# Three score buffers and one working bank in an attention and coupling block

## The reference

```
q, k, v, g = x @ Wq.T, x @ Wk.T, x @ Wv.T, x @ Wg.T      # 16 query heads, 4 key/value groups, head size 8
v = v * sigmoid(g);  q, k = rms_norm(q), rms_norm(k);  q, k = rotary(q), rotary(k);  q = q * q_gain
for s in (first half of the head, second half):           # head size 4 each
    a[s] = softmax(causal(q[s] @ k[s].T / 2)) @ v[s]
y = concat(a[0] - lam * a[1], a[0] + lam * a[1])
x = layernorm(x + y @ Wo.T)                               # over all 16 sequences
gf = global_net(mean of x over the tokens)                # three small dense layers
out = x
for _ in range(3):
    tf = coupling_net(out)                                # dense 128-128-64-32-1, gelu, sigmoid at the end
    out = out + (0.1 + adaptive_range * (0.7 * gf + 0.3 * tf - 0.5) * 2) * twist(out)
result = layernorm(x + out)
```

## Time and profile before

| | before |
|---|---|
| median of three runs | 305.38 us (305.05, 305.38, 306.28) |
| the profiled execution | 305.05 us |
| its span, first to last instruction | 303.2 us |
| TensorE matmuls busy | 270.1 us |
| ScalarE busy | 237.7 us |
| VectorE busy | 199.9 us |
| GpSimd busy | 82.4 us |
| mean granted TensorE clock | 0.991 |

### The profile page before, as it was taken

One profiled execution on the slowest core, in us unless ns is written; L12 is line 12 of the kernel. 1 busy time (PEld: TensorE's weight loads), 2 busy tenths in 40 slices (PEclk: granted clock), 3 DMA queues, 4 the chain that ended last, 5 costly groups with the idle time before them and its releaser, 6 DMA issues.

```text
span 303.2 us, 8211 instructions
## 1 busy us (share of the span) xinstructions
PE 270.1 (89%) x2888; PEld 119.0 (39%) x2888; DVE 199.9 (66%) x764; ACT 237.7 (78%) x337; POOL 82.4 (27%) x241
## 2 busy tenths in 40 slices
PE   4069899999999999999999999999998999998990
PEld 3042343434434344344443444434343322222890
DVE  5577467676676765767657677563244567799884
ACT  2158889898898988989889898897875777776565
POOL 6331231513315133141431414321011000042263
PEclk9999999999999999999999999999999999999996
DMA  4204235161442506426053340632200156533025
GB/s 107 64 1 91 53 67 105 41 138 27 94 97 78 104 19 136 89 49 139 17 104 82 81 98 17 121 75 53 64 0 1 45 132 138 125 85 69 27 76 177
DMA packets 56918, 23.40 MB, mean 77 GB/s; under 512 B 42656, under 2 KB 53824, under 8 KB 56896
## 3 DMA queue, kind: packets, MB, share of 16 engines
q1 hardware_dynamic: 56896, 23.12, 34.2%
HBM read 4.90 MB, written 2.10 MB: 23 GB/s over the span
## 4 chain that ended last, share of the span: by engine, by line
PE 45%; DVE 25%; ACT 13%; issue 11%; POOL 2%; DMA 1%; DVEq 0%; POOLq 0%; SPq 0%; ACTq 0%
PE S L661 6%; PE MA L373 5%; ACT probs_past L809 5%; PE O L560 5%; PE O L553 5%; PE S L448 5%; PE MA L586 3%; PE S L487 3%; DVE cY L1246 3%; DVE square L988 2%; PE S L478 2%; DVE turned L997 2%; ACT probs_late L809 2%; DVE heads L1110 2%; ACT qkvg L787 2%
## 5 line engine op out<-in xcount | busy, mean ns | idle before, releaser
L809 ACT ACTIVATE probs_late<-S 128x1024 f32<-128x1024 f32 x64 | 62.5, 1038 | 8.2 <-PE S L458 8.2
L809 ACT ACTIVATE probs_past<-S 128x1024 f32<-128x1024 f32 x64 | 62.1, 1024 | 6.4 <-PE S L448 5.2
L809 ACT ACTIVATE probs_early<-S 128x1024 f32<-128x1024 f32 x32 | 31.0, 1021 | 8.4 <-PE S L487 8.4
L547 PE MATMUL O<-probs_past,values 128*32 128x512 f32 x256 | 34.5, 611 | 0.7
L553 PE MATMUL O<-probs_late,values 128*32 128x256 f32 x512 | 34.3, 385 | 0.0
L1342 POOL TENSOR_TENSOR minus_half_sum<-sum_eps,minus_half 128x40 f32<-128x40 f32 x16 | 4.3, 268 | 104.2 <-DVE estimate L1016 104.2
L1025 DVE TENSOR_TENSOR roped<-rotated,rstd 128x128 f32<-128x128 f32 x64 | 12.2, 250 | 30.9 <-POOL rstd L1357 30.9
L1246 DVE SCALAR_TENSOR_TENSOR cY<-coup,ratio,Y 128x256 f32<-128x256 f32 x48 | 25.1, 565 | 7.9 <-ACT coup L891 7.9
L458 PE MATMUL S<-qk 32*64 32x256 bf16 x512 | 29.4, 292 | 0.9 <-ACT probs_past L809 0.4
L661 PE MATMUL S<-X,cn_w 128*128 128x512 f32 x48 | 25.3, 629 | 1.0 <-DVE X L1252 1.0
L373 PE MATMUL MA<-w_proj,xT_in 128*128 128x224 f32 x64 | 18.9, 424 | 4.5 <-DMA xT_in<-in_xT 3.9
(11 more groups left out here) (172 smaller groups left out, 544.4 us busy)
## 6 DMA issues: line engine op xcount, KB each, us to landing
Y<-X SPq DMA_DIRECT2D x48, 128.0 KB, 2.3
xT_in<-in_xT SPq DMA_DIRECT2D x16, 128.0 KB, 2.5
x_res<-in_x SPq DMA_DIRECT2D x16, 128.0 KB, 2.1
out<-result SPq DMA_DIRECT2D x8, 256.0 KB, 2.3
qk<-parts SPq DMA_TRANSPOSE x15, 4.9
future_in<-in_future SPq DMA_DIRECT2D x1, 128.0 KB, 2.1
w_o<-in_w_o SPq DMA_DIRECT2D x2, 64.0 KB, 2.0
cn_w<-in_cn_w SPq DMA_DIRECT2D x2, 64.0 KB, 2.4
```

What stands on the lines that cost most here:

```text
L547: mm = pe.matmul(O[32 * g:32 * g + 32, :], values[p][:, 0, g, s, at:at + 32], probs_past[:, s, g, :], start=m == 0, stop=False)
L809: act.activation(dst, S[n % 2][:, :, :], ACT.Exp).then_inc(exp_done[n], 1)
```

## The change

The score tiles get a third buffer of two banks, S[2]. `TILE_BUFFER` gives each of the ten tiles its buffer and `TILE_BEFORE` the tile whose exponential has to be done before the buffer is written. The banks MA, MB and MC give way: one bank M now takes, in turn, the projection of b + 2, the turned x1 of b - 2, the turned outputs, the turned heads and the output projection of b - 1. In the stages before and after the batches MB and MA are names for the two halves of S[2], and MC for M.

A late pair is written together: both far parts, both masks, both near parts (`late_pair`). On TensorE turning x1 comes behind late pair 4, turning the outputs behind late pair 6, turning the heads behind the early pair, and the output projection behind weighing 3, at the end of the batch. Turning x1 also waits for the sum of its own batch and for the copy of the projection, turning the outputs for that copy. On ScalarE the copy of the projection comes one exponential earlier, the keeping of x1 one later, the tanh one later, and the copy of the heads one later. On VectorE the heads are normalized before the values are gated. The output projection's reader, `add_residual`, and the next projection keep their places.

```
+TILE_BUFFER = (0, 1, 2, 0, 1, 2, 0, 1, 0, 2)
+TILE_BEFORE = (8, 7, 9, 0, 1, 2, 3, 4, 6, 5)
...
-        S = [ps(f"S{i}", [128, 2, R * 128]) for i in range(2)]
+        S = [ps(f"S{i}", [128, 2, R * 128]) for i in range(3)]
         O = ps("O", [128, R * 128])
-        MA = ps("MA", [128, 512])
-        MB = ps("MB", [128, 512])
-        MC = ps("MC", [128, 512])
...
+        M = ps("M", [128, 512])
+        MB, MA, MC = S[2][:, 0, :], S[2][:, 1, :], M[:, :]
...
             def bank_free(b, n):
 
-                if n >= 2:
-                    pe.wait_ge(exp_done[n - 2], b + 1)
+                before = TILE_BEFORE[n]
+                if before < n:
+                    pe.wait_ge(exp_done[before], b + 1)
                 else:
-                    reach(pe, exp_done[len(TILES) - 2 + n], b)
+                    reach(pe, exp_done[before], b)
...
+            def late_pair(b, p, n):
+
+                for m in (n, n + 1):
+                    bank_free(b, m)
+                for m in (n, n + 1):
+                    late_part(p, m, True)
+                for m in (n, n + 1):
+                    late_mask(m)
+                for m in (n, n + 1):
+                    late_part(p, m, False).then_inc(scores_done[m], 1)
...
-            def turn_outputs(b):
+            def turn_outputs(b, project_more, bank=M):
 
                 pe.wait_ge(n_["o_ready"], b + 1)
                 reach(pe, n_["X0_ready"], b if not isinstance(b, int) or b < BATCH - 1 else b - 1)
+                if project_more:
+                    pe.wait_ge(n_["qkvg_ready"], b + 4)
...
-            def turn_x1(b, bank=MB):
+            def turn_x1(b, project_more, bank=M):
 
                 pe.wait_ge(n_["x1_ready"], b + 1)
+                reach(pe, n_["summed_done"], b + 1)
+                if project_more:
+                    pe.wait_ge(n_["qkvg_ready"], b + 5)
...
                 weigh(b, p, 0)
-                late_first(b, p, 4)
+                late_pair(b, p, 4)
                 if not first and not second:
-                    turn_x1(b - 2)
-                late_rest(b, p, 4)
+                    turn_x1(b - 2, project_more)
                 weigh(b, p, 1)
+                late_pair(b, p, 6)
                 if not first:
-                    turn_outputs(b - 1)
-                late_first(b, p, 6)
-                late_rest(b, p, 6)
+                    turn_outputs(b - 1, project_more)
                 weigh(b, p, 2)
-                if not first:
-                    turn_heads(b - 1, project_more)
                 early_pair(b, p, 8)
                 if not first:
+                    turn_heads(b - 1)
+                weigh(b, p, 3)
+                if not first:
                     output_projection(b - 1)
-                weigh(b, p, 3)
...
                 exponentials(b, 2)
-                exponentials(b, 3)
                 if project_more:
                     copy_projection(b + 2, p)
+                exponentials(b, 3)
+                exponentials(b, 4)
                 if not first and not second:
                     keep_x1(b - 2)
-                exponentials(b, 4)
                 exponentials(b, 5)
+                exponentials(b, 6)
                 if project_more:
                     gate_tanh(b + 2, p)
-                exponentials(b, 6)
                 exponentials(b, 7)
+                exponentials(b, 8)
                 if not first:
                     copy_heads(b - 1)
-                exponentials(b, 8)
                 exponentials(b, 9)
...
+                if not first:
+                    normalize_heads(b - 1)
                 if not last:
                     gate_values(b + 1, 1 - p)
-                if not first:
-                    normalize_heads(b - 1)
```

More of the change, by code:

```diff
@@ L217, in block_kernel @@
         result = sb("result", [128, 4, 4, DIM])
-        S = [ps(f"S{i}", [128, 2, R * 128]) for i in range(2)]
+        S = [ps(f"S{i}", [128, 2, R * 128]) for i in range(3)]
         O = ps("O", [128, R * 128])
-        MA = ps("MA", [128, 512])
-        MB = ps("MB", [128, 512])
-        MC = ps("MC", [128, 512])
[L225 to L228, removed]
+        M = ps("M", [128, 512])
+        MB, MA, MC = S[2][:, 0, :], S[2][:, 1, :], M[:, :]
+        Z_BANKS = (MB, MA, O[:, :], MC)
+        BACK_BANKS = (S[0][:, 0, :], S[0][:, 1, :], S[1][:, 0, :], S[1][:, 1, :], MB, MA, O[:, :], MC)
+        TURN_BANKS = (S[2][:, 0, :].bitcast(BF16), S[2][:, 1, :].bitcast(BF16))
+        MAX_BANKS = (S[1][:, 0, :], S[1][:, 1, :])
+        MAX_TURN_BANKS = tuple(bank.bitcast(BF16) for bank in MAX_BANKS)
         names = ("w_proj_loaded gain_loaded trig_loaded ident_future_loaded w_out_loaded ffn_loaded tables_ready zeros_ready biases_halved "
@@ L372, in project, with turn_queries @@
                 for t in range(T):
-                    mm = pe.matmul(MA[:, t * PROJ:(t + 1) * PROJ], xT_in[p][:, t * 128:(t + 1) * 128], w_proj[:, :],
+                    mm = pe.matmul(M[:, t * PROJ:(t + 1) * PROJ], xT_in[p][:, t * 128:(t + 1) * 128], w_proj[:, :],
                                    start=True, stop=True)
                 mm.then_inc(n_["proj_done"], 1)
-            def turn_queries(b, t, parts_in="parts_ready", turned="turned"):
+            def turn_queries(b, t, parts_in="parts_ready", turned="turned", banks=TURN_BANKS):
                 pe.wait_ge(n_[parts_in], b + 1)
-                if t == 1:
-                    reach(pe, n_["heads_done"], b - 1)
-                bank = (MC16, MB16)[t]
+                bank = banks[t]
                 for n in range(R * 2):
@@ L395, in turn_keys @@
                     u = NQ + n * G
-                    mm = pe.transpose(MC16[:, n * 128:(n + 1) * 128],
+                    mm = pe.transpose(TURN_BANKS[0][:, n * 128:(n + 1) * 128],
                                       parts[:, u:u + G, :, :].rearrange("p u s d -> p (u s d)"), ident16[:, :])
@@ L420, in blocks_for_maximum @@
                         r, s = n // 2, n % 2
-                        bank = (MB, MC)[n % 2]
+                        bank = MAX_BANKS[n % 2]
                         for g in range(G):
@@ L467, in late_mask @@
                         rows = halves((j + h) % 2)
-                        pe.matmul(S[n % 2][halves(1 - t), j, t * 256:(t + 1) * 256], future16[rows, 0, rows], one_edge(rows, R),
+                        pe.matmul(S[TILE_BUFFER[n]][halves(1 - t), j, t * 256:(t + 1) * 256], future16[rows, 0, rows], one_edge(rows, R),
                                   start=False, stop=True)
@@ L477, in early_part @@
                             rows = group_rows(2 * h + j)
-                            pe.matmul(S[n % 2][halves(t), j, s * 256:(s + 1) * 256], kT[p][rows, t, s, halves(t)],
+                            pe.matmul(S[TILE_BUFFER[n]][halves(t), j, s * 256:(s + 1) * 256], kT[p][rows, t, s, halves(t)],
                                       qT[p][rows, t, :, s, halves(t)], start=s == 0, stop=False)
@@ L486, in early_mask @@
                         rows = halves((j + h) % 2)
-                        mm = pe.matmul(S[n % 2][halves(t), j, :], future16[rows, 0, rows], one_edge(rows, 2 * R),
+                        mm = pe.matmul(S[TILE_BUFFER[n]][halves(t), j, :], future16[rows, 0, rows], one_edge(rows, 2 * R),
                                        start=False, stop=True)
@@ L786, in copy_projection, with keep_x1 @@
                 reach(act, n_["values_ready"], b - 1)
-                act.activation(qkvg[p][:, :, :].rearrange("p t c -> p (t c)"), MA[:, 0:T * PROJ], ACT.Copy)\
+                act.activation(qkvg[p][:, :, :].rearrange("p t c -> p (t c)"), M[:, 0:T * PROJ], ACT.Copy)\
                    .then_inc(n_["qkvg_ready"], 1)
-            def keep_x1(b, bank=MB):
+            def keep_x1(b, bank=M):
                 at = b * SEQ
@@ L929, in _ @@
             gelu1(0, 1)
-            copy_heads(BATCH - 1)
+            copy_heads(BATCH - 1, MA)
             gelu2(0, 0)
@@ L1100, in subtract_maximum, with normalize_heads @@
                 dve.memset(parts[:, 0:NQ, 6, 0:3], 0.0)
-            def normalize_heads(b):
-                turned_o = MB[:, :].rearrange("p (n c) -> p n c", c=32)[:, :, 0:4 * OUTROW]\
+            def normalize_heads(b, bank=M):
+                turned_o = bank[:, :].rearrange("p (n c) -> p n c", c=32)[:, :, 0:4 * OUTROW]\
                     .rearrange("p n (w c) -> p n w c", c=OUTROW)
```

65 lines of the change are left out of this document (27 added, 38 removed).

## The result

| | before | after |
|---|---|---|
| median | 305.83 us (4 runs, 305.05 to 308.24) | 288.48 us (4 runs, 288.27 to 288.74) |
| ratio to before, 95% interval | | 0.940 (0.935 to 0.944) |
| span of the profiled execution | 303.2 us | 286.6 us |
| one steady batch | 12.72 us | 11.63 us |

The account below looks back on a forecast made before the run. TensorE was taken to bound each batch: 12.72 - 11.65 = 1.07, times 16 = 17.1 us, from 305.05 to 288.0; jitter made it 288.8, and 0.33 for the median 289. Range 286 to 298.

Parts of the forecast that it names:

- TensorE bounds, and work taken from it shows: Steady batch: TensorE busy 12.44 of 12.72 us, so issuing or waiting less shortens it, to 11.65.
- The late pair, 0.82: TensorE's late score tiles: three groups instead of five, 0.82 (0.72 to 0.95) against 1.18, saving 0.72 a batch.
- the early masks' 0.56: Early pair's eight masks of 512 columns: 0.56 taken as evidence that two mask groups share one drain.
- The walk through the waits: One new batch stepped through all engines with trace prices: next batch at 11.65, one wait of 0.17 staying.
- the wait that it named: TensorE before weighing 0, which needs the output bank copied by ScalarE: 0.17 a batch.
- The third buffer: Score tiles: no tile waits for the exponential that frees its buffer, though the first two margins are 0.1.
- only the waits go: Rival: no TensorE group gets cheaper, batch 12.37, 299 to 300 us; chance 0.08.
- The single bank M: Bank shared by projection, x1, outputs, heads and output projection: ScalarE's copies out of it are done before TensorE wants them.
- the slow rival: Bank M: each ScalarE copy slips behind one more exponential (0.92), batch 13.46, 317 us; chance 0.04.
- The ring of x1: Turning x1, output projection, VectorE's sum and x1: 11.47 a batch, margin 0.18; x1 late gives 293, chance 0.12.
- The ends: First and last batches: 0.9 to 1.3 gained, SyncE's transpose a batch ahead of use, front stage unchanged.
- The 0.8 added for jitter: Batches where three engines' cycles nearly tie: 0.05 a batch from the spread of exponentials, raising 288.0 to 288.8.

Follow-up runs that it names:

- the tile-by-tile kernel: Changed kernel with late pairs written one tile after the other again, three buffers, bank M and new order kept: 296.88 us, ratio 0.964.
- the fastest kernel: Changed kernel with both past pairs written earlier, the sum of x1 moved ahead of the split and x1 normalized inside the split: 283.52 us, ratio 0.923.
- The table of the kernels: Batch times: three buffers, merged late pairs 11.63, unmerged 12.19; two buffers, merged 14.79, unmerged 13.45; kernel before 12.72 us.
- past pair early: Changed kernel with the next batch's first past pair written ahead of the output projection: 289.68 us, ratio 0.946.
- the kernel with the second past pair first: Changed kernel with first past pair ahead of output projection, sum of x1 moved, second past pair ahead of the projection: 286.82 us, ratio 0.933.

## Why the prediction was right

**TensorE bounds, and work taken from it shows.** Right. The steady batch was forecast at 11.65 and is 11.63. Of the 1.07 to be gained the forecast had 0.72 as work and 0.35 as waits; of the 1.09 gained 0.68 was work and 0.41 waits.

**The late pair, 0.82.** Right, 0.84, and the mask group is the 0.34 that was interpolated, not the 0.24 or 0.47 of its bounds. That it shows in the batch is what the tile-by-tile kernel confirms, less the 0.12 that its longer pair hides. The prediction took the early masks' 0.56 as siding with one fixed cost for both tiles' masks. That row alone did not tell the rules apart: 0.20 for each tile and 0.04 for each round give 0.24 and 0.56 as well, and would have made the merged masks 0.48. The measured 0.34 decides it.

**The walk through the waits.** Right about the wait that it named, blind to a second one, and off in several prices; that the total came out within 0.02 is luck, as the errors cancel. At weighing 0 the wait is 0.36 (116.40 + 0.32 to 117.08) and not 0.17, and 0.12 more stand at weighing 1, which the walk did not hold against exponential 3, though the change itself puts the copy of the projection ahead of that exponential. Against this, a past pair costs 0.32 (114.12 to 114.44) and not 0.40, the length of its row, twice; the turning of heads 0.37 (123.73 to 124.10) and not 0.47; and turning x1 0.36 without its wait, not 0.45. Both turnings were priced from start distances in the kernel before, and each of these held a wait: the group behind x1 started at 114.28, and exponential 3, for which it waits, ended at 114.22; the group behind the heads started at 119.47, and exponential 7 ended at 119.33. The late pairs are 0.03 over. In sum +0.31 for waits and -0.33 for work. TensorE's own batch is thus 11.15 and not 11.48, and the fastest kernel bears it out: 11.20, with 0.05 of waits left.

**The third buffer.** Its place in the argument was right and its weight understated. The prediction priced "only the waits go" at 0.35 a batch and the merging at 0.72, as parts that add. The table of the kernels shows that they do not: with two buffers the same merging costs 1.34.

**The single bank M.** Right: in the steady batch no step of TensorE waits for a copy out of it, and the slow rival did not come. ScalarE has no idle time before any of its three copies out of M.

**The ring of x1.** The forecast had 0.24 between the end of x1 and its turning, 0.18 without the 0.06 of a semaphore; the trace has 0.20, 0.14 without. 0.33 more on VectorE shows as a wait there, and 0.33 less changes nothing, until TensorE gets shorter.

**The ends.** Here one statement failed: the prediction had SyncE's transposing DMA a batch ahead of use, and each batch of the ends 0.9 to 1.3 shorter. Batch 0 gained 0.06 (from 11.87 to 11.81), since batch 1 starts like this:

```profile
32.59 0.40 PE L448 MATMUL S<-qk 32*128 32x512 bf16 x4 [1.07 <-DMA qk<-parts]
```

The parts of batch 1 are made while batch 0 runs, not a batch ahead. Their DMA is issued at 25.88 (25.66 before) and lands 6.7 us later, at 32.6, so batch 1 cannot start earlier (32.44 before). Batch 1 then gained 1.67 (13.29 to 11.62), more than forecast. Twelve steady batches gave 1.08 each, the last two 1.05 and 1.14: 0.06 + 1.67 + 12.96 + 1.05 + 1.14 = 16.9, less 0.2 for a start that is 0.2 later, 16.7. The 0.8 added for jitter has no counterpart in the trace. It was taken off a gain of 17.1, and the gain was 16.7: the 0.4 that was lost went at the front and not through jitter, so this term came near by luck.

## What to carry to other kernels

Where TensorE is full, count its groups of matmuls by form, not its matmuls: here joining two tiles' groups saved a whole group (0.24) where the matmuls had different places, and 0.13 of one where they shared them, but it paid only with buffers that let both tiles be written at once. A price read as the distance between two starts can hold a wait that no bracket shows, so hold each step against everything that it waits for. Before an order is changed, walk one period through every engine and note each margin; a ring with 0.1 to 0.2 us of slack bounds as soon as the longest one is shortened, so that an edit that removes the visible wait (past pair early) loses by itself and wins only with the edits that shorten the next ring.

## What the runs showed of the hardware

Four and eight 32x64 matmuls of 256 columns, each on a place of its own, cost the same, 0.24 us from start to start (0.25 in the changed kernel). Masks on the same four 64x64 places cost 0.24 for four, 0.34 for eight (118.32 to 118.66), and 0.55 for eight of 512 columns (123.18 to 123.73). So a further round of 256 columns on the same places is 0.10, and the 0.13 that is left of a group is there once, however many rounds it has. For the 32x64 matmuls a second round on the same places is 0.13 (the early pair's sixteen take 0.37, 122.81 to 123.18). The Trainium skill, TensorEngine Tiling (Array Packing), Key Properties, has the engine drain when the tiling mode changes. The 0.34 agrees with one drain for both tiles' masks, but no run here tells a drain from another fixed cost of a group.

The length of an exponential of one size is not constant. With two buffers, where ScalarE often waits for scores, those of the late tiles lasted 1.01 to 1.03 us; in the changed kernel, where they follow each other without a wait, up to 1.11, and up to 1.14 in the kernel with the second past pair first. The next instruction still started 0.90 to 0.95 behind the start in the batches shown here, so only who waits for the end of one, as weighing 1 does, pays for it. What makes the end later was not tried.
